# A bilinear-interaction recommendation tower on one core: a new rule for the order of all work

## What is computed

```python
e = jnp.stack([tbl_f[ids[:, f]] for f in range(32)], axis=1)   # 1024 x 32 x 64
left = jnp.einsum('bpd,pde->bpe', e[:, idx_i, :], W)           # W: 496 x 64 x 64
z = jnp.sum(left * e[:, idx_j, :], axis=-1)                    # 1024 x 496
h = jnp.concatenate([z, dense_ctx], axis=1)                    # 1024 x 512
h = jnp.maximum(h @ W_top1 + b_top1, 0.0)                      # 512 -> 512
h = jnp.maximum(h @ W_top2 + b_top2, 0.0)                      # 512 -> 256
y = h @ W_top3                                                 # 256 -> 1
```

## Time and profile before

| | us |
|---|---|
| median of 3 runs (lowest to highest) | 521.97 (518.9 to 523.16) |
| the profiled execution, its own time | 518.04 |
| its span, first to last instruction | 516.2 |
| PE busy | 412.0 (80% of the span) |
| DVE busy | 345.1 (67%) |
| ACT busy | 337.1 (65%) |
| POOL busy | 246.2 (48%) |
| mean granted TensorE clock | 0.96 of full speed |

### The profile page before, as it was taken

One profiled execution on the slowest core, in us unless ns is written; L12 is line 12 of the kernel. 1 busy time (PEld: TensorE's weight loads), 2 busy tenths in 40 slices (PEclk: granted clock), 3 DMA queues, 4 the chain that ended last, 5 costly groups with the idle time before them and its releaser, 6 DMA issues.

```text
span 516.2 us, 8890 instructions
## 1 busy us (share of the span) xinstructions
PE 412.0 (80%) x2440; PEld 211.9 (41%) x2440; DVE 345.1 (67%) x301; ACT 337.1 (65%) x2584; POOL 246.2 (48%) x266
## 2 busy tenths in 40 slices
PE   0173299999599679998799779998796979998597
PEld 0110154543245335643344535534252545543244
DVE  0042068899497486699877467799687548799660
ACT  0053336679785676779995467699985347699902
POOL 6777777777777777777107777770000000000000
PEclk9999979999799899999999899999899889999989
DMA  7999913111111111111001111110000000000000
GB/s 136 167 172 169 163 27 99 28 28 29 27 27 28 27 25 30 29 27 30 8 1 27 28 27 26 31 26 7 0 2 2 1 1 1 2 0 2 2 0 0
DMA packets 44679, 18.86 MB, mean 37 GB/s; under 512 B 39764, under 2 KB 40280, under 8 KB 44632
## 3 DMA queue, kind: packets, MB, share of 16 engines
q1 hardware_dynamic: 36120, 8.86, 13.1%
q0 software_dynamic: 8512, 9.45, 8.4%
HBM read 18.29 MB, written 0.00 MB: 35 GB/s over the span
## 4 chain that ended last, share of the span: by engine, by line
PE 43%; ACT 33%; DVE 8%; POOL 7%; issue 7%; DMA 2%; DVEq 0%; ACTq 0%
ACT row_products L505 31%; PE left L611 14%; PE z_sum L637 8%; PE left L616 7%; POOL rows L412 7%; PE turned L655 4%; DVE row_products L459 4%; PE turned L667 3%; PE turned L573 2%; PE left L624 2%; DVE column_products L451 2%; PE left L655 1%; ACT X L487 1%; DVE z_nat L468 1%; DMA rows<-in_tbl_dram,ids_sb 1%
## 5 line engine op out<-in xcount | busy, mean ns | idle before, releaser
L505 ACT ACTIVATE row_products<-row_products 128x64 f32<-128x64 f32 x1248 | 298.4, 244 | 49.0 <-DVE row_products L459 49.0
L412 POOL DMA_INDIRECT rows<-in_tbl_dram,ids_sb x256 | 241.7, 944 | 101.3 <-issue 77.4
L505 ACT ACTIVATION_READ_ACCUMULATOR row_products<-row_products 128x1 f32 x1248 | 237.1, 190 | 0.0
L459 DVE TENSOR_TENSOR row_products<-left,rows 128x1024 f32<-128x1024 f32 x120 | 144.9, 1218 | 94.4 <-PE left L616 87.6
L616 PE MATMUL left<-w_sb,X 64*128 64x512 f32 x480 | 137.5, 656 | 12.1 <-DVE row_products L459 4.1
L451 DVE TENSOR_TENSOR column_products<-left,X 128x1024 f32<-128x1024 f32 x104 | 124.9, 1215 | 31.2 <-PE left L611 31.1
L611 PE MATMUL left<-X,w_sb 64*128 64x256 f32 x960 | 133.8, 405 | 8.9 <-DVE row_products L459 5.9
L611 PEld LDWEIGHTS left<-X,w_sb 64*128 64x128 f32 x960 | 90.5, 194 | 69.5 <-DVE row_products L459 28.4
L573 PE MATMUL turned<-ident,rows 128*128 128x128 f32 x128 | 26.2, 317 | 53.8 <-DMA rows<-in_tbl_dram,ids_sb 37.9
L637 PE MATMUL z_sum<-column_products,ones_window 128*32 128x512 f32 x512 | 65.8, 631 | 0.0
L616 PEld LDWEIGHTS left<-w_sb,X 64*128 64x128 f32 x480 | 42.3, 195 | 55.4 <-DVE row_products L459 26.0
(11 more groups left out here) (26 smaller groups left out, 59.5 us busy)
## 6 DMA issues: line engine op xcount, KB each, us to landing
rows<-in_tbl_dram,ids_sb POOLq DMA_INDIRECT x256, 2.4
w_sb<-in_W_top_dram SPq DMA_DIRECT2D x1, 512.0 KB
w_sb<-in_L_rec_W_dram SPq DMA_DIRECT2D x1, 496.0 KB, 10.8
w_sb<-in_L_rec_W_dram SPq DMA_DIRECT2D x1, 480.0 KB, 11.2
w_sb<-in_L_rec_W_dram SPq DMA_DIRECT2D x1, 464.0 KB, 10.9
w_sb<-in_L_rec_W_dram SPq DMA_DIRECT2D x1, 448.0 KB, 10.7
w_sb<-in_L_rec_W_dram SPq DMA_DIRECT2D x1, 432.0 KB, 10.2
w_sb<-in_L_rec_W_dram SPq DMA_DIRECT2D x1, 416.0 KB, 10.9
```

The costliest lines, as they stand in the source:

```text
L412: pool.indirect_dma_start(out=rows[:, q % 2 * QT + t, f * D:(f + 1) * D], out_offset=None, in_=tables[f], in_offset=bass.IndirectOffsetOnA ...
L459: nc.vector.tensor_tensor(row_products[:, n % ROW_PRODS, :, :], left[:, s, :, :], rows[:, t:t + 1, 2 * D * c:2 * D * (c + 4)].to_broadcast ...
L505: ins = nc.scalar.activation(product, product, ACT.Copy, accum_out=z_nat[:, tile, column:column + 1])
```

## The change

`merged`, `column_slots`, `summed_by_dve` and the fixed places are gone. `make_work` gives two lists for all quarters, the column pieces (own pieces among them) and the row pieces. A class `Order` walks through time with a clock for PE, DVE and ACT, a cost in us for each step, and the times at which gathers and W are taken to arrive. At each step it asks when an X batch, a batch of sums, an MLP step, the next row piece and the next column piece could begin, and takes the one that can begin soonest, within a small tolerance in that order of preference; between a row and a column piece it takes the stream that is behind in its share. A row sum is given to ACT if ACT is free within 0.5 us, else to DVE if it fits ahead of the next multiply, else it waits. MLP steps stand at least three pieces apart where they claim the bank. `make_plan` then adds the end and the two "wT" steps, which `Order` doesn't know.

In the first quarter POOL gathers both tiles of a field pair before the next field pair, and X batches always hold both tiles (10 batches in place of 19, for 32 transposes as before). `COLUMN_PRODS` goes from 7 to 6 and `ROW_PRODS` from 4 to 5. What each step computes is unchanged. Lines that are only "..." are left out.

```diff
@@ -34,20 +34,19 @@
 RING = 3
 LAG = 2
 TURN = 8
-COLUMN_PRODS = 7
-ROW_PRODS = 4
-
-
-FIRST_BATCHES = [4, 2] + [1] * 10
-SECOND_BATCHES = [4, 2, 2, 2, 2, 2, 2]
-
-X_AHEAD = 6
-X_APART = 4
-
-MLP_AT = [("zT", 5), (("layer1", 0), 10), (("layer1", 1), 11), (("layer1", 2), 17), (("layer1", 3), 18),
-          (("layer2", 0), 25), (("layer2", 1), 26), (("layer3", 0), 32)]
-
-EARLY = range(10, 3, -1)
+COLUMN_PRODS = 6
+ROW_PRODS = 5
+
+BATCHES = [2, 2, 2, 1, 1, 1, 1, 2, 2, 2]
+
+MLP_STAGES = [("zT", 0), ("layer1", 0), ("layer1", 1), ("layer1", 2), ("layer1", 3), ("layer2", 0), ("layer2", 1), ("layer3", 0)]
+MLP_APART = 3
+
+
+WORK, OWN, SUM, SET, TRANSPOSE, LAYER, SWITCH, RELOAD = 0.87, 1.85, 0.215, 0.15, 0.12, 1.72, 0.1, 0.12
+MULTIPLY, ROWSUM_DVE, ROWSUM_ACT, COPY, RELU, SIGNAL = 1.23, 1.23, 3.9, 0.6, 0.47, 0.12
+GATHER, LANDING, W_FIRST, W_PAIR = 5.0, 9.5, 6.0, 0.1
+ACT_SLACK, DVE_SLACK, MARGIN, NEAR, LAST_LEAD = 0.5, 0.6, 1.0, 0.3, 0.15
...
@@ -80,23 +79,16 @@
-def merged(a, b):
-
-    placed = [((i + 0.5) / len(c), x) for c in (a, b) for i, x in enumerate(c)]
-    return [x for _, x in sorted(placed, key=lambda p: p[0])]
-
-
 def make_work():
 
 
-    work = [("rows", 0, 0, m, c) for m in EARLY for c in row_chunks(m)]
-    begin = {}
+    columns, rows = [], []
     for q in range(QUARTERS):
         single = None
         for m in range(FP - 1, -1, -1):
-            begin[q, m] = len(work)
             ks = column_groups(m)
-            columns = []
+            if m % 8 == 0:
+                columns.append(("own", q, m))
             if len(ks) % 2:
                 if single is None:
                     single = (m, ks[-1])
@@ -105,17 +97,12 @@
                     single = None
                 ks = ks[:-1]
             columns += [("columns", q, ((m, k), (m, k + 1))) for k in reversed(ks[::2])]
-            rows = [("rows", q, QT * q + t, m, c) for c in row_chunks(m) for t in range(QT)]
-            rows = [x for x in rows if x not in work[:len(EARLY)]]
-            if m % 8 == 0:
-                columns.insert(0, ("own", q, m))
-            work += rows + columns if (q, m) == (QUARTERS - 1, 0) else merged(rows, columns)
-    return work, begin
-
-
-def column_slots():
-
-    return [w for w in make_work()[0] if w[1] == 0 and w[0] != "rows"]
+            rows += [("rows", q, QT * q + t, m, c) for c in row_chunks(m) for t in range(QT)]
+    return columns, rows
...
-def summed_by_dve(n, rows_in_all):
-
-    return n % 3 == 0 or n >= rows_in_all - 2
...
+def make_batches():
+
+    batches = []
+    for q in range(QUARTERS):
+        m = FP
+        for n in BATCHES if q == 0 else [2] * (FP // 2):
+            batches.append((q, list(range(m - 1, m - 1 - n, -1))))
+            m -= n
+    return batches
+
+class Order:
+    def __init__(self):
+        self.columns, self.rows = make_work()
+        self.batches = make_batches()
+        self.plan, self.work = [], []
+        self.pe = self.dve = self.act = self.bank = 0.0
+        self.fill, self.held = None, False
+        self.end = []
+        self.left = [0.0] * RING
+        self.column_work, self.row_work, self.waiting = [], [], []
+        self.row_end, self.sum_end, self.z_end = {}, {}, {}
+        self.sums = self.batch = 0
+        self.x_ready = {}
+        self.mlp, self.stage, self.mlp_ready, self.mlp_work = 0, 0, 0.0, -99
+        self.w_ready, t = {}, W_FIRST
+        for m in range(FP - 1, -1, -1):
+            t += (2 * (F - 1 - 2 * m) - 1) * W_PAIR
+            self.w_ready[m] = t
+    def done(self, q):
+        return len(self.column_work) >= COLUMN_PIECES * (q + 1) and len(self.row_work) >= ROW_PIECES * (q + 1)
+    def landed(self, q, m):
+        if q < 2:
+            return GATHER * (FP * q + FP - m) + LANDING
+        if not self.done(q - 2):
+            return None
+        begin = max(GATHER * FP * q, max(e for e, x in zip(self.end, self.work) if x[1] == q - 2))
+        return max(begin + GATHER * (FP - m), GATHER * (FP * q + FP - m)) + LANDING
+    def on_pe(self, what, begin, length):
+        late = begin > self.pe + 0.01
+        self.pe = max(begin, self.pe) + (SWITCH if what != self.fill else RELOAD if late else 0) + length
+        self.fill = what
+    def on_act(self, length):
+        self.act = max(self.act, self.pe + SIGNAL) + length
+        return self.act
+    def by_act(self, n):
+        self.act = max(self.act, self.end[self.row_work[n]] + SIGNAL) + ROWSUM_ACT
+        self.row_end[n] = self.act
+        self.plan += [("rowsum0", self.row_work[n]), ("rowsum1", self.row_work[n])]
+    def by_dve(self, n):
+        self.dve = max(self.dve, self.end[self.row_work[n]] + SIGNAL) + ROWSUM_DVE
+        self.row_end[n] = self.dve
+        self.plan.append(("rowsum", self.row_work[n]))
+    def sum_rows(self, now, limit):
+        while self.waiting:
+            ready = self.end[self.row_work[self.waiting[0]]] + SIGNAL
+            if max(self.act, ready) <= now + ACT_SLACK:
+                self.by_act(self.waiting.pop(0))
+            elif max(self.dve, ready) + ROWSUM_DVE <= limit + DVE_SLACK:
+                self.by_dve(self.waiting.pop(0))
+            else:
+                return
+    def force_rows(self):
+        n = self.waiting.pop(0)
+        ready = self.end[self.row_work[n]] + SIGNAL
+        (self.by_dve if max(self.dve, ready) + ROWSUM_DVE <= max(self.act, ready) + ROWSUM_ACT else self.by_act)(n)
+    def x_candidate(self):
+        if self.batch < len(self.batches) and not self.held:
+            q, fields = self.batches[self.batch]
+            rows = self.landed(q, fields[-1])
+            if rows is not None:
+                return max(rows, self.bank) + SIGNAL
+        return None
+    def sum_candidate(self):
+        a = self.sums // 2
+        if a + TURN // 2 > len(self.column_work) or self.end[self.column_work[a + TURN // 2 - 1]] + SIGNAL > self.pe + NEAR:
+            return None
+        q = self.sums // SUMS
+        return max(self.pe, self.z_end[q - 1] + SIGNAL) if self.sums % SUMS == 0 and q else self.pe
+    def mlp_candidate(self):
+        q = self.mlp
+        if q == QUARTERS or q == QUARTERS - 1 and self.stage:
+            return None
+        what, n = MLP_STAGES[self.stage]
+        if what == "zT":
+            rows = ROW_PIECES * (q + 1)
+            if len(self.row_work) < rows or any(r < rows for r in self.waiting):
+                return None
+            ready = max(self.row_end[r] for r in range(rows))
+        elif (what, n) == ("layer1", 0):
+            if q not in self.z_end:
+                return None
+            ready = max(self.z_end[q], self.mlp_ready)
+        else:
+            ready = self.mlp_ready
+        if n % 2 == 0:
+            if len(self.work) - self.mlp_work < MLP_APART:
+                return None
+            ready = max(ready, self.bank)
+        return max(ready + SIGNAL + NEAR, self.pe)
+    def column_candidate(self):
+        n = len(self.column_work)
+        if n == len(self.columns) or n >= COLUMN_PRODS and 2 * (n - COLUMN_PRODS) + 1 not in self.sum_end:
+            return None
+        kind, q, of = self.columns[n]
+        ms = [m for m, k in of] if kind == "columns" else range(of, of + 8)
+        if (q, min(ms)) not in self.x_ready:
+            return None
+        ready = max(self.x_ready[q, min(ms)], self.left[len(self.work) % RING]) + SIGNAL
+        return max([self.pe, ready] + [self.w_ready[m] for m in ms])
+    def row_candidate(self):
+        n = len(self.row_work)
+        if n == len(self.rows):
+            return None
+        q, m = self.rows[n][1], self.rows[n][3]
+        if (q, m) not in self.x_ready or q > len(self.column_work) // COLUMN_PIECES + 1 or q - 2 >= self.mlp and self.stage == 0:
+            return None
+        ready = max(self.x_ready[q, m], self.left[len(self.work) % RING]) + SIGNAL
+        if n >= ROW_PRODS:
+            if n - ROW_PRODS not in self.row_end:
+                return None
+            ready = max(ready, self.row_end[n - ROW_PRODS] - WORK)
+        return max(self.pe, ready, self.w_ready[m])
+    def take_x(self, begin):
+        q, fields = self.batches[self.batch]
+        self.on_pe("x", begin, SET + 2 * len(fields) * TRANSPOSE)
+        self.plan.append(("x", self.batch))
+        self.bank = self.on_act(COPY)
+        for m in fields:
+            self.x_ready[q, m] = self.bank
+        self.batch += 1
+    def take_sum(self, begin):
+        self.on_pe("sum", begin, TURN * SUM)
+        for v in range(self.sums, self.sums + TURN):
+            self.plan.append(("sum", v))
+            self.sum_end[v] = self.pe
+        self.sums += TURN
+        if self.sums % SUMS == 0:
+            self.z_end[self.sums // SUMS - 1] = self.on_act(COPY)
+    def take_mlp(self, begin):
+        what, n = MLP_STAGES[self.stage]
+        self.on_pe("x", begin, {"zT": SET + 4 * TRANSPOSE, "layer3": LAYER / 2}.get(what, LAYER))
+        self.plan.append((what, self.mlp if what == "zT" else (self.mlp, n)))
```

(132 more changed lines are left out.)

79 lines of the change are left out of this document (2 added, 77 removed).

## The result

The changed kernel takes 437.82 us (median of 4 runs, 437.62 to 438.33), the kernel before 520.43 (4 runs). The ratio is 0.8413, with a 95% interval of 0.8364 to 0.8461. The profiled execution has a span of 436.1 us and a granted clock of 0.98. The number forecast was 438, and it is hit better than its terms are, as the part on the prediction shows.

What follows compares the result with a forecast made beforehand. No engine was full, so order lost the time; PE would become the steady bound. 128 + 96 + 96 + 97 + 16.7 = 433.7 us of span, 435.5 as execution, 438 as median; range 418 to 470 for 8 in 10.

Steps and rivals of the forecast that it cites:

- T0: End of the first quarter: 128 us, bounds 123 and 140, from 48 DVE units at 1.41 us after 58.8 us.
- the share of 95%: Busy share assumed for the bounding engine: DVE in the first quarter, PE in the steady ones, where 90.5/0.95 = 95.3 us.
- the two wT steps: First quarter: two steps put in without a place in the time model, could cost 0 to 9 us; 1.5 taken.
- The steady quarters: Quarters after the first: PE becomes the bound, DVE and ACT close behind; period 96 us, bounds 91.5 and 113, last 97.
- The sum of 90.5 us of PE content: PE's work in one steady quarter, added up from distances between starts of its pieces, sums, batches and layer steps: 90.5 us.
- the sum by it, 413.5: Total if PE is judged by weight loads, 51.7 of 112.9 us: ample PE room, DVE and ACT set about 89 us.
- 34 to 38 row sums on DVE: Sign expected if the forecast held: 34 to 38 of the kernel's row sums done on DVE.
- POOL's wait: POOL's 22.04 us wait for the end of the second quarter goes; gathers then bound only the first quarter.
- The tail: Stretch behind the fourth quarter's last multiply: 16.7 us, the kernel before's value, added to the sum.
- The step from one execution to the median: Median of runs taken as 0.76% above the profiled execution: 435.5 x 1.0076 = 438.8 us.
- ACT as the bound: Steady quarters: ACT takes 23 of 30 row sums, periods of 105 us, median 467 us; chance 0.22.
- rival 4: Slower: finer mix gives PE many small waits and it stays at 1.2 GHz; from 527 us, periods of 125.5; chance 0.06.

Runs made afterwards that it cites:

- d1: Kernel before with only the first quarter's start changed: both tiles of a field pair gathered together, X batches of both tiles, no early row pieces; 503.2 us.
- u1: Changed kernel with the old fixed rule for row sums, every third on DVE and the others on ACT, whichever is idle; 464.9 us.
- n2: Changed kernel, same list, with layer 1 of the first three quarters using two of its four input chunks, 11.5 us less PE work; 434.9 us.
- u2c: Changed kernel with row and column pieces in the old single merged order, blocking row sums placed first; 454.56 us.
- u3: Changed kernel with each MLP step forced in at its old fixed place, ready or not; 743.76 us, on the disturbed chip alone.
- i1b: Changed kernel with the early half of the last layer 1 working on the column sums, moved ahead of the row sums' transposition; 432.82 us.
- n1: Changed kernel, same list, with each row sum on ScalarE summing 8 of its 16 column groups, some 150 us less ACT work; 439.09 us.

## Why the prediction was right, and where it was not

- **The first quarter** (T0 = 128): it ended at 127.2. The way there was less exact: the 16th multiply ended at 63.5 and not at 58.8, and the other 48 took 63.7 us, 1.33 each and not 1.41, with DVE busy for 59.78 of 63.70 us, 94%. So the share of 95% was right and the price of a unit, 1.34 us, too high: it took DVE to do 10 row sums in this quarter as before, and it did 5. For the two wT steps 1.5 us were added; PE has no wait for their copies of W in the changed kernel's list of waits. d1 shows that the new start in the old list gives only 139.5, and u1 gives 141.6; this pace needed the free choice of engine as well.
- **The steady quarters** (96, 96, 97): 94.7, 96.7 and 94.7. The sum of 90.5 us of PE content and the share of 95% fit the length. The reason given, that PE would be the bound, holds only in part, and this is a step of the mechanism that the runs don't bear out: n2 took out 11.5 us of PE's work and 2.9 came back. DVE, put at 84.4 us a period, was busy for 87.5 in the first two, since it had 12 row sums in each and not 9. Weight loads take 49.5 of 94.66 us now. By the rule of the Trainium skill that I had weighed ("Perfetto Trace Analysis", section "Identifying the Most-Contended Engine") PE would still have much room; the sum by it, 413.5, was 24 us too low.
- **34 to 38 row sums on DVE**: wrong, 42 as before. The new rule did not change how many, but which and when: by the same cuts in the traces 5, 12, 12, 10 and 3, where it was 10, 10, 10, 12 and 0. That this is worth 27.0 us (u1), 14.4 of them in the first quarter, was in no term of my sum; for the steady quarters I had put the gain on the spread of row pieces, which is worth 16.7 in all (u2c), and on the distance between MLP steps. Old places for these cost some 2 us in the one quarter that can be read (u3).
- **POOL's wait** of 22 us: gone, as worked out.
- **The tail** (16.7): 22.8. This step failed. I took it over unchanged, though in the new order the last piece is a row piece and its sum the last input, and "early" stands behind "zT" and works on those sums. PE waited 6.27 us and then did both halves of layer 1, 8.94 us, in place of one; i1b, which moves the early half, gave 5.0 us back.
- **The step from one execution to the median**: I multiplied by 1.0076, 3.3 us. The profiled execution after is 436.1 + 1.84 = 437.9 us and the median 437.82, so nothing was to be added.
- The errors cancel: the first quarter was put 0.8 too long, the periods 2.9 in sum, the step to the median 3.3, and the tail 6.1 too short; 0.8 more went by saying 438 for 438.8. That the total is right to 0.2 us is luck.
- **Rivals.** ACT as the bound (467): n1 rules it out. u1 comes near its time, 464.9, but has such a period only once: 105.6 us with ACT busy for 98.50, and 96.5 and 97.2 after it. The clock (rival 4): granted 1.00 in all steady windows. The swinging clock that the Trainium skill tells of for slot cycling ("TensorE: Matmul & The Clock Gate", section "A second HAM failure mode: psum-queue depth-cycling") again doesn't show here; clock is lost in the first 63.5 us (0.92), where PE waits for gathers, and behind the 6.27 us wait, 0.85 in the tail's window.

## What to carry to other kernels

Where no engine is full but each is at times, ask what makes the full stretches: a fixed share of work per engine can be right in the sum and wrong in single stretches. Choosing the engine at each step was worth 27.0 us here and the spread of the pieces 16.7; in the steady quarters the two were about equal, 13.2 and 12.3. After reordering, look at the end anew: whichever input used to be early may now be the late one. And when a profile shows one engine busy for 98%, take work away from it before calling it the bound; here a quarter of what was taken came back.

## What was not expected of the hardware

On one chip the same kernels took 744 to 803 us, and 796 for the kernel before. The traces have nearly the same durations for the same instructions (a multiply of row pieces 1219 ns in both u3 and the changed kernel, a gather 947 and 944), but for long stretches in which POOL gathers, the other engines hardly run. Windows of u3 there, with gathers and without:

```profile
283.00:363.00 80.00, 4.22 (x16) 2.13 (x16) 3.82 (x4) 5.73 (x33) 53.17 (x57) 0.53 0.13 23
363.00:448.00 85.00, 83.12 (x508) 46.00 (x508) 73.98 (x64) 71.78 (x552) 3.77 (x4) 0.96 0.01 3
```

In 80 us of gathering PE is busy for 4.22, then for 83.12 of 85.00 without it. The changed kernel has 73 gathers in 96.74 us, much the same rate as the 57 in these 80 us, beside a PE at 98%. The longest waits are for no instruction that the profile shows, such as this one of TensorE in u3:

```profile
94.47 3.78 PE L754 MATMUL left<-w_sb,X 64*128 64x512 f32 x8 [54.24 <-issue]
```

What these engines wait for stays open. The changed kernel itself was not run there; u3, the nearest to it, has a ratio of 0.9331 to the kernel before on that chip. That this is because gathers and work hardly overlap there is likely and was not tested.
